# Adding the two expert outputs of each token on TensorE instead of VectorE

## The reference

```python
x = x + _L0_gnn_ref(_layernorm(x), W, src, dst, edge_weight)   # graph convolution
x = x + _L0_ffn_ref(_layernorm(x)[None], ...)[0]               # attention, then 64 experts, top 2
x = x + _L1_gnn_ref(_layernorm(x), edge_index, W_l, ...)       # mean over neighbours, batch norm
x = x + _L1_ffn_ref(_layernorm(x)[None], ...)[0]               # 8 experts, top 2
```

```python
# end of _L0_ffn_ref: each token sums the outputs of its two experts, weighted by its gates
y = einsum('ecf,efh->ech', h, w2) + b2[:, None, :]
ys = y[ef, posc] * (gf * keep)[:, None]
moe_out = ys.reshape(T, TOP_K, H).sum(axis=1)
return x + moe_out
# start of _L1_gnn_ref, on the normalized rows: mean over the incoming edges
agg = segment_sum(x[src], dst);  mean_nb = agg / maximum(deg, 1)[:, None]
h = relu(mean_nb @ W_l.T + b_l + x @ W_r.T)
```

## Time and profile before

| | |
|---|---|
| median of 3 runs | 1349.58 us |
| the profiled execution's own time | 1349.58 us |
| its span, first to last instruction | 1347.7 us |
| PE busy | 1287.8 us (96%) |
| DVE busy | 740.6 us (55%) |
| ACT busy | 454.8 us (34%) |
| PE's mean granted clock | 0.979 of full speed |

### The profile page before, as it was taken

The page is one execution under the profiler, slowest core; times in us unless marked ns, Lnnn a source line. Parts: engine busy times, 40 slices in busy tenths (PEclk is TensorE's granted clock), DMA queues, the critical chain, the costliest instruction groups (busy, mean ns, idle before and its releaser), DMA issues. The chain is left out here.

```text
span 1347.7 us, 23141 instructions
## 1 busy us (share of the span) xinstructions
PE 1287.8 (96%) x7703; PEld 865.5 (64%) x7704; DVE 740.6 (55%) x1605; ACT 454.8 (34%) x1127; POOL 350.6 (26%) x491
## 2 busy tenths in 40 slices
PE   9999999999989999999999999999989999899991
PEld 4799954455447777777756677777745555566660
DVE  6699965572148788878767333333366001373334
ACT  2599930021035555555512111111151002441110
POOL 4499920000000000000021555555410000224540
PEclk9999999999999999999998999999989999989996
DMA  6000000040010000000061799999840043232326
GB/s 169 32 2 3 2 1 1 0 191 0 0 43 2 1 1 2 2 1 1 1 196 47 252 331 320 324 321 315 266 167 0 1 137 113 94 100 86 101 87 241
DMA packets 83548, 133.31 MB, mean 99 GB/s; under 512 B 11952, under 2 KB 49222, under 8 KB 82687
## 3 DMA queue, kind: packets, MB, share of 16 engines
q1 hardware_dynamic: 69491, 110.29, 24.9%
q0 software_dynamic: 12176, 18.68, 4.5%
q10 hardware_dynamic: 1788, 3.16, 0.7%
HBM read 117.41 MB, written 29.56 MB: 109 GB/s over the span
## 5 line engine op out<-in xcount | busy, mean ns | idle before, releaser
L1281 POOL TENSOR_TENSOR b_x<-b_x,b_r 125x512 f32<-125x512 f32 x10 | 12.7, 1267 | 526.4 <-DVE b_r L1741 526.4
L1360 PEld LDWEIGHTS ps<-b_r 128*128 128x128 f32 x1024 | 124.2, 192 | 33.8 <-issue 32.2
L1360 PE MATMUL ps<-b_r 128*128 128x78 f32 x1024 | 122.2, 272 | 1.2 <-DVE b_r L1723 1.2
L1369 PE MATMUL ps<-b_r 128*78 128x512 f32 x256 | 120.3, 592 | 0.0
L660 PE MATMUL ps<-b_r 125*125 125x160 f32 x660 | 117.2, 314 | 0.1
L569 ACT ACTIVATE b_r<-b_r 125x125 f32<-125x125 f32 x330 | 106.8, 390 | 0.4 <-issue 0.2
L1625 ACT ACTIVATE b_r<-ps,b_r 128x78 f32<-128x78 f32 x128 | 34.8, 323 | 203.0 <-PE ps L1360 183.8
L1029 PEld LDWEIGHTS ps<-b_r 125*64 125x64 f32 x1600 | 85.3, 136 | 24.6 <-issue 22.8
L992 PE MATMUL ps<-b_r 64*125 64x417 f32 (+1 forms) x480 | 95.5, 530 | 1.4 <-DVE ps L1121 1.2
L1453 PE MATMUL ps<-b_r 125*128 125x417 f32 (+1 forms) x240 | 89.3, 525 | 7.1 <-DVE b_r L217 7.1
L1029 PE MATMUL ps<-b_r 125*64 125x125 f32 x1600 | 94.7, 272 | 1.3 <-ACT b_r L1057 1.3
(11 more groups left out here) (283 smaller groups left out, 2251.9 us busy)
## 6 DMA issues: line engine op xcount, KB each, us to landing
b_r<-L_ffn_w SPq DMA_DIRECT2D x128, 512.0 KB
b_r<-y SPq DMA_DIRECT2D x20, 512.0 KB, 7.5
b_r<-L_ffn_W SPq DMA_DIRECT2D x2, 4096.0 KB, 20.0
y<-b_r SPq DMA_DIRECT2D x2, 2500.0 KB
rows<-b_r SPq DMA_DIRECT2D x4, 960.0 KB
b_x<-x SPq DMA_DIRECT2D x5, 480.0 KB
out<-b_x ACTq DMA_DIRECT2D x5, 480.0 KB
b_r<-L_ffn_b SPq DMA_DIRECT2D x1, 2048.0 KB, 9.3
```

Of the source, the lines that this page charges most:

```text
L1360: last = pe.matmul(T.ps[:, 2 + r % 2, f * CAP:(f + 1) * CAP], T.ew1[r % WS][:, k, f * 128:(f + 1) * 128], T.ex_t[:, r % 2, k, :], start=(k ...
L1369: last = pe.matmul(T.ps[:CAP, 4 + r % 2, :], T.eh[:, r % 2, f, :], T.ew2[r % WS][:, f, :], start=(f == 0), stop=(f == FK - 1))
```

## The change

Instead of two scalar_tensor_tensor of DVE per tile, ACT makes two diagonal matrices per tile, with the gates of the 125 tokens on the diagonal (`gate_matrices`: the identity scaled by a column of `T.gate`). PE multiplies each with the tile of expert outputs of that choice; both products add up in one bank of PSUM. DVE adds that bank to `x` once. Banks 0 and 1 take turns for these sums, and there are two buffers of diagonals.

The bias matmuls now use banks 6 and 7 in turn, in place of the table `BIAS`, so the third and every later one waits until DVE has added the one two before it. ACT makes the diagonals of tiles 0 and 1 ahead, then in each turn one tile of counts, one root and the diagonals of the tile two ahead. PE does the early sums of tile t-2 after the expert sum of tile t. A function `gated_sum` is added that nothing calls.

```diff
+def gate_matrices(act, T, t, before, ready):
+    if t >= 2:
+        act.wait_ge(before, t - 1)
+    for j in range(TOP):
+        last = act.activation(T.diagonal[:, t % 2, j, :], T.ident[:P, :P], ACT.Copy, scale=T.gate[:, t, j:j + 1])
+    last.then_inc(ready, 1)
...
-    BIAS = (6, 7, 4, 5, 0, 1, 2, 3, 0, 1)
...
             pe.wait_ge(S.b2_loaded, 16)
+            pe.wait_ge(S.wl_copied, 2)
             for t in range(NT):
-                if t < 8:
-                    pe.wait_ge(S.wl_copied, banks.index(BIAS[t]) + 1)
-                else:
-                    pe.wait_ge(S.bias_added, t - 3)
-                pe.matmul(T.ps[:P, BIAS[t], :], T.gates_t[:, t * P:(t + 1) * P], T.b2_rows, start=True, stop=True)\
+                if t >= 2:
+                    pe.wait_ge(S.bias_added, t - 1)
+                pe.matmul(T.ps[:P, 6 + t % 2, :], T.gates_t[:, t * P:(t + 1) * P], T.b2_rows, start=True, stop=True)\
                   .then_inc(S.bias_done, 1)
...
-            for k in range(NT):
-                early_sums(k)
+            for t in range(NT):
+                if t >= 2:
+                    pe.wait_ge(S.moe_added, t - 1)
+                pe.wait_ge(S.diagonals_ready, t + 1)
+                pe.wait_ge(S.y_gathered[t // 2], 32)
+                for j in range(TOP):
+                    last = pe.matmul(T.ps[:P, t % 2, :], T.diagonal[:, t % 2, j, :], choices[j][:, t, :],
+                                     start=(j == 0), stop=(j == TOP - 1))
+                last.then_inc(S.moe_done, 1)
+                if t >= 2:
+                    early_sums(t - 2)
+            early_sums(NT - 2)
+            early_sums(NT - 1)
...
-            EARLY_COUNTS = 6
-            for t in range(EARLY_COUNTS):
-                counts(t)
+            for t in range(2):
+                gate_matrices(act, T, t, S.moe_done, S.diagonals_ready)
+            counts(0)
             for t in range(NT):
+                if t + 1 < NT:
+                    counts(t + 1)
                 row_roots(act, T, S, 2, [t])
-                if t + EARLY_COUNTS < NT:
-                    counts(t + EARLY_COUNTS)
+                if t + 2 < NT:
+                    gate_matrices(act, T, t + 2, S.moe_done, S.diagonals_ready)
...
-            def choice(t, j):
-                dve.wait_ge(S.y_gathered[t // 2], 32)
-                return dve.scalar_tensor_tensor(out=T.x[:, t, :], in0=choices[j][:, t, :], scalar=T.gate[:, t, j:j + 1],
-                                                in1=T.x[:, t, :], op0=ALU.mult, op1=ALU.add)
+            def add(t):
+                dve.wait_ge(S.moe_done, t + 1)
+                dve.tensor_tensor(T.x[:, t, :], T.ps[:P, t % 2, :], T.x[:, t, :], ALU.add).then_inc(S.moe_added, 1)
+                dve.wait_ge(S.moe_added, t + 1)
+                row_moments(dve, link, T, T.x, t, S.rows_var)
...
             for t in range(NT):
-                bias(t)
-            dve.wait_ge(S.bias_added, NT)
-            for t in range(NT):
-                link(choice(t, 0))
-                link(choice(t, 1))
-                row_moments(dve, link, T, T.x, t, S.rows_var)
+                add(t)
                 if t > 0:
                     normalized(t - 1)
```

More of the change, by code:

```diff
@@ L849, in load_expert, with gated_sum @@
       .then_inc(S.ew_loaded[slot], 16)
+def gate_matrices(act, T, t, before, ready):
[4 more added lines that the diff above has]
+    last.then_inc(ready, 1)
+def gated_sum(pe, T, t, bank, gates_t, biases, rows):
+    pe.matmul(T.ps[:P, bank, :], gates_t[:, t * P:(t + 1) * P], biases, start=True, stop=False)
+    for j in range(TOP):
+        last = pe.matmul(T.ps[:P, bank, :], T.diagonal[:, t % 2, j, :], rows[j][:, t, :], start=False, stop=(j == TOP - 1))
+    return last
 def projections(nc, T, S, A):
@@ L1776, in _ @@
             output(LOOPS, (E0 - 1) - WS * LOOPS)
-            def bias(t):
+            for t in range(NT):
                 dve.wait_ge(S.bias_done, t + 1)
-                dve.tensor_tensor(T.x[:, t, :], T.ps[:P, BIAS[t], :], T.x[:, t, :], ALU.add).then_inc(S.bias_added, 1)
-            def choice(t, j):
-                dve.wait_ge(S.y_gathered[t // 2], 32)
-                return dve.scalar_tensor_tensor(out=T.x[:, t, :], in0=choices[j][:, t, :], scalar=T.gate[:, t, j:j + 1],
-                                                in1=T.x[:, t, :], op0=ALU.mult, op1=ALU.add)
+                dve.tensor_tensor(T.x[:, t, :], T.ps[:P, 6 + t % 2, :], T.x[:, t, :], ALU.add).then_inc(S.bias_added, 1)
+            dve.wait_ge(S.bias_added, NT)
+            def add(t):
[3 more added lines that the diff above has]
+                row_moments(dve, link, T, T.x, t, S.rows_var)
             def normalized(t):
@@ L1987, in semaphores_by_name @@
     S.wl_turned, S.wl_copied, S.moe_added = semaphores("wl_turned wl_copied moe_added")
-    [S.conv_rows] = semaphores("conv_rows")
+    S.diagonals_ready, S.moe_done, S.conv_rows = semaphores("diagonals_ready moe_done conv_rows")
     S.ct_ready, S.means_ready, S.sums_done = semaphores("ct_ready means_ready sums_done")
@@ L2161, in program @@
         T.ct_f = r34[:P, 0:NT * N].rearrange("p (k n) -> p k n", k=NT)
+        T.diagonal = r5[:P, 2 * KD * D:2 * KD * D + 2 * TOP * P].rearrange("p (b j q) -> p b j q", b=2, j=TOP)
         T.feats = feats_of(r2)
```

## The result

Over ten runs the changed kernel takes 1357.1 us (1355.46 to 1360.09), the kernel before 1349.32 us (1346.49 to 1352.85) in ten runs beside it. The ratio is 1.0055, with an interval of 1.0043 to 1.0068: 7.4 us slower (5.8 to 9.2). The two medians lie 7.8 us apart. The forecast was 1360.2 us in a range of 1356.5 to 1363.

A forecast was written before the change was run, and what follows sets the result against it. DVE was taken to bound about 32 us of the stage, PE everything behind. New stage 0.7 + 17.2 + 28.0 + 1.4 = 47.3 against 38.4 us, +8.9, with the clock's 1.7 +10.6: 1360.2 us, range 1356.5 to 1363.

The forecast's parts named there:

- PE takes the stage over: Stage from bias to last early sum: 17.2 us of expert sums exceed PE's 10.4 us to spare, so PE bounds it.
- The signs that the prediction named: In the stage: one PE idle time of 1.4 us, L1487 at 0.43 us each, DVE waits of some 2 us a tile.
- The main term: Expert sums on PE at L1487: 20 matmuls at 0.86 us each, 17.2 us.
- DVE's gain is worth nothing: DVE's round falls from 3.23 to 2.40 us, but PE's is 4.52 us, so DVE waits and nothing is gained.
- The bias in two banks: Bias matmuls wait for DVE's add two before: four rounds, 0.7 us, bounds 0 and 1.4 us.
- The late diagonals: Before tile 2's expert sum, PE waits once for ACT's diagonals: 1.4 us, bounds 0 and 2 us.
- the lower bound of 0 for this term: The wait before tile 2's expert sum was allowed to cost as little as 0 instead of 1.4 us.
- rival 1: Same stage without the fall of PE's clock: +8.9 us, 1358.5 us; 1357.1 without the wait before tile 2; chance 0.28.
- The clock: Short PE idle times in the stage bring 3.4 us at half clock: 1.7 us lost, bounds 0 and 3.4.
- The whole shift arrives at the end: Behind the stage PE bounds without a break and all hangs on `sums_done`, so the full +10.6 us reaches the end.

The follow-up runs named there:

- e3: The changed kernel with the first matmul of each expert sum done twice, 30 matmuls instead of 20; 1366.0 us, ratio 1.0133.
- e4: The kernel before, DVE and ACT work untouched, plus 20 unread PE matmuls of the expert sums' shape at the same places; 1357.2 us, ratio 1.0078.
- e7: The changed kernel freed of waits: bias in four banks, expert sums three tiles ahead, three banks, four buffers of diagonals; 1355.4 us, ratio 1.0041.
- the hybrid: The kernel before with expert sums of tiles 1 to 4 (or 1 to 3) on PE ahead of the first early sum; 1344.2 us (or 1346.6 us).
- e2: The changed kernel with the bias matmuls in four banks instead of two; 1353.3 us, ratio 1.0046.
- e5: The changed kernel with two more ACT counts between the root of tile 0 and the diagonals of tile 2; 1365.8 us, ratio 1.0122.
- e1: The changed kernel with a third buffer of diagonals, so those of tile 2 are made ahead; 1358.3 us, ratio 1.0070.
- e6: The changed kernel with only the first choice on PE, DVE adding the second, 10 matmuls instead of 20; 1355.1 us, ratio 1.0042.
- e9: The kernel before with 28 unread bf16 matmuls keeping PE busy behind the bias, before the first early sum; 1349.0 us, ratio 1.0002.

## Why the prediction was right, step by step

**PE takes the stage over.** Right, and this is the cause. The profile after shows PE's round of 4.52 us, e3 the price of each matmul, and e4 that the matmuls alone, without any relief of DVE, make a loss of the same size. e7 splits it: 6.9 of the 9.1 us are PE's work beyond what it had to spare, 2.2 us are waits. The signs that the prediction named are there: one idle time of PE in the stage, a pace of 0.43 us at L1487, waits of 2.04 us before DVE's add in a steady round.

**The main term, 20 matmuls for 17.2 us.** Right: four instructions take 1.72 us in every round. The figure of 131 ns that the Trainium skill gives for a matmul of 512 columns in a sustained stream (page "TensorE: Matmul & The Clock Gate", section "Back-to-back issue gap") would by the prediction's estimate have made this 10.5 us. The trace does not agree: 1.72 us in every round, and no run shows less.

**DVE's gain is worth nothing.** Right in the changed kernel (e4). In the hybrid the same 0.83 us a tile are worth their full amount (43.9, 44.7 and 47.2 us for four, three and no tiles), since there DVE is still the bound, and with four tiles just level with PE.

**The bias in two banks, 0.7 us.** It was 0.75 (9.53 against 8.78), and e2 gives 0.8 back.

**The late diagonals, 1.4 us.** The size and the place are right: PE ended tile 1 at about 999.7 and started tile 2 at 1001.09. The chain names DVE's L1816 for this wait. But DVE's add of tile 0, for which PE waits by the program, ended at 999.03. ACT's rows name the true one:

```profile
1000.20 0.20 ACT L210 ACTIVATE b_std<-b_spread 125x1 f32<-125x1 f32 x1 [7.70 <-DVE b_spread L203]
1000.31 0.68 ACT L857 ACTIVATE b_r<-b_ident,b_gate 125x125 f32<-125x125 f32 x2
```

They end at 1000.99, and PE starts 0.1 us later; e5 moved them and PE went along. What I had wrong is the lower bound of 0 for this term, on which "1357.1 us without the late diagonals" in rival 1 rests: the first normalized tile is the next to be late, and e1 gets 0.2 us back, not 1.4. I had worked out that this tile would be there when PE came to it, but not what that was worth if PE came earlier.

**The clock, 1.7 us.** This is the step that failed. The clock stayed at 1.00 in the whole stage, so by the trace rival 1 is what happened: its +8.9 us stand against 9.1 measured. The forecast's 1360.2 is 3.1 us above the measured 1357.1; by this trace 1.7 of it is this term. The rest is that the whole time grew by less than the stage (below). The mechanism exists in this stage (e4, e5, e6), but 1.4 us of idle time did not set it off in this kernel's profiled execution. Read in the same view as the idle times of the earlier trace rows it is 1.14 us, as long as the one in 719.0 to 720.6, which was followed by a fall before. Whether the clock fell in this stage in the other ten runs, which were not profiled, is not known. The two banks of the bias did not set it off either: the trace shows 1.00 through and behind eight waits of PE for DVE. By the section "A second HAM failure mode: psum-queue depth-cycling" of the Trainium skill's page "TensorE: Matmul & The Clock Gate", as the prediction read it, the clock would have swung there. This trace does not agree, with 1.00 in each stretch.

**The whole shift arrives at the end.** Right by the profile (310.7 and 310.8 us behind the stage). The 7.4 us by which the whole time grew are less than the 9.1 of the stage, but their interval ends at 9.2. Whether anything outside the stage gives back a microsecond stays open: behind the stage the traces of all runs lie between 310.6 and 312.4 us, which is as large a difference as the one in question.

## What to carry to other kernels

Work moved from the bounding engine to another is free only inside the other's idle time. Add up, for the stage alone, what that engine does at full clock, and move no more than the rest. Count with it that the relief makes the stage shorter: here 10.4 us were to spare and 17.2 us were moved, while the four tiles of the hybrid take 6.9 us and shorten the stage by 3.3, which uses up 10.2. A fifth tile was not run; by an estimate from the same rows PE would then need 8.8 + 8.6 + 28.0 = 45.4 us, more than the 43.9 with four. Put the moved work where the idle time lies, here ahead of the first early sum. e6 moved only 8.6 us, but into each round, and lost 6.

## What the runs showed of the hardware

Behind short idle times of PE its clock fell from 2.4 to 1.2 GHz or did not, and the same place in the same code does both. Before, it fell at 275.96 and was down at 724 to 726; in the changed kernel's trace neither is there. Of the twelve traces, whose code is the same up to there, seven have a mean clock of 0.57 to 0.61 from 276 to 280 us, and five have 1.00. An idle time of 0.78 us was followed by a fall (e4), one of 1.14 us in the changed kernel and one of 1.13 in e2, in the same view, were not, and in one of 3.40 us (e5) the clock fell before PE went on, and was down for 6.8 us. In the stage the falls cost 1.0 us (e4), about 1.6 (e6) and 3.1 (e5). They go with the spread between runs of one kernel: of eleven runs of the changed kernel the fastest, 1355.46 us, had a mean clock of 0.985 and the slowest, 1360.09 us, one of 0.982. By an estimate from these numbers 0.003 less is 8 us at half clock and 4 us lost, against 4.6 measured.

In a stage bound by another engine the same half clock costs nothing (e9: 1.00 in place of 0.51, 47.2 us both times).
